# Feed-forward products in plain fp32 with one operand each, instead of fp32r high and low parts

## What is computed

```python
W_in_sim = quantize_w8_per(W_in, axis=0)      # round to 8 bit steps, one scale for each column
W_out_sim = quantize_w8_per(W_out, axis=1)    # one scale for each of the 1024 rows
x_sim = quantize_a16(x)                       # round to 1/32767 of the largest |x|
hidden = gelu(x_sim @ W_in_sim + b_in)        # 256 -> 1024
hidden_sim = quantize_a16(hidden)             # needs the largest |hidden| of all
out = hidden_sim @ W_out_sim + b_out          # 1024 -> 256
```

## Time and profile before

| | |
|---|---|
| median of 3 runs | 2500.81 us (2496.88 to 2504.37) |
| span of the profiled execution | 2491.9 us |
| TensorE busy | 1955.9 us, 78% |
| VectorE busy | 1747.3 us, 70% |
| ScalarE busy | 1316.8 us, 53% |
| GpSimd busy | 797.0 us, 32% |
| F0 | about 867 to 999 us |
| G0 | about 2109 to 2293 us |
| G1 | about 2293 to 2492 us |

### The profile page before, as it was taken

One profiled execution on the slowest core, in us unless ns is written; L12 is line 12 of the kernel. 1 busy time (PEld: TensorE's weight loads), 2 busy tenths in 40 slices (PEclk: granted clock), 3 DMA queues, 4 the chain that ended last, 5 costly groups with the idle time before them and its releaser, 6 DMA issues. The chain is left out here.

```text
span 2491.9 us, 47293 instructions
## 1 busy us (share of the span) xinstructions
PE 1955.9 (78%) x14240; PEld 1576.1 (63%) x14240; DVE 1747.3 (70%) x3674; ACT 1316.8 (53%) x2381; POOL 797.0 (32%) x866
## 2 busy tenths in 40 slices
PE   1689999999999679277788777887777775786687
PEld 0567777777777467255666666666666663665676
DVE  6567778877877378465667767767666665676788
ACT  0255666656655378144444444444444443786676
POOL 3012222222222200423333333333333332221787
PEclk9899999999999689578888888888888877898899
DMA  5576887888878100356665656666666661356565
GB/s 164 107 157 145 169 172 162 166 169 166 170 161 165 53 3 0 76 104 122 123 120 116 117 109 116 119 112 118 111 118 122 121 118 54 135 220 252 196 242 186
DMA packets 259781, 333.54 MB, mean 134 GB/s; under 512 B 29152, under 2 KB 237184, under 8 KB 251520
## 3 DMA queue, kind: packets, MB, share of 16 engines
q1 hardware_dynamic: 233088, 277.00, 49.4%
q0 software_dynamic: 26624, 55.67, 9.6%
HBM read 185.70 MB, written 144.70 MB: 133 GB/s over the span
## 5 line engine op out<-in xcount | busy, mean ns | idle before, releaser
L610 DVE TENSOR_REDUCE L_negm<-L_s_bank 128x2 f32<-128x512 f32 x1024 | 684.4, 684 | 363.2 <-PE L_s_bank L418 360.7
L475 ACT ACTIVATE L_prob<-L_t_bank 128x512 f32<-128x512 f32 x1024 | 598.9, 598 | 631.8 <-PE L_t_bank L429 625.7
L418 PE MATMUL L_s_bank<-L_kst,L_qst 96*128 96x256 f32 x2048 | 526.1, 343 | 236.5 <-DMA L_kst<-k_scratch 176.7
L418 PEld LDWEIGHTS L_s_bank<-L_kst,L_qst 96*128 96x128 f32 x2048 | 355.4, 216 | 363.0 <-issue 142.0
L429 PE MATMUL L_t_bank<-L_qst,L_kst 98*128 98x256 f32 x2048 | 460.6, 311 | 18.3 <-ACT L_prob L475 15.2
L429 PEld LDWEIGHTS L_t_bank<-L_qst,L_kst 98*128 98x128 f32 x2048 | 361.7, 217 | 33.3 <-ACT L_prob L475 30.0
L339 PE MATMUL L_o_bank<-L_prob,L_vext 128*32 128x256 f32 x4096 | 301.1, 415 | 2.7 <-ACT L_prob L475 2.7
L1289 PE MATMUL G_acc<-G_w_out,G_hhl 128*128 128x256 f32 x1024 | 140.4, 291 | 59.4 <-DVE G_hhl L1259 59.1
L259 POOL DMA_DIRECT2D L_den<-o_scratch x64 | 35.5, 554 | 452.2 <-DMA o_scratch<-L_osb 452.2
L1289 PEld LDWEIGHTS G_acc<-G_w_out,G_hhl 128*128 128x128 f32 x1024 | 127.9, 192 | 72.1 <-DVE G_hhl L1259 37.5
L339 PEld LDWEIGHTS L_o_bank<-L_prob,L_vext 128*32 128x32 f32 x4096 | 112.5, 115 | 92.6 <-issue 18.8
(11 more groups left out here) (172 smaller groups left out, 3257.2 us busy)
## 6 DMA issues: line engine op xcount, KB each, us to landing
L_qst<-q_scratch SPq DMA_DIRECT2D x384, 128.0 KB, 5.0
L_kst<-k_scratch SPq DMA_DIRECT2D x384, 128.0 KB, 6.4
q_scratch<-L_qhl SPq DMA_DIRECT2D x64, 512.0 KB, 3.0
k_scratch<-L_khl SPq DMA_DIRECT2D x64, 512.0 KB, 3.2
o_scratch<-L_osb POOLq DMA_DIRECT2D x128, 256.0 KB, 4.8
hidden_scratch<-G_hid SPq DMA_DIRECT2D x32, 1024.0 KB, 3.9
G_hid<-hidden_scratch SPq DMA_DIRECT2D x32, 1024.0 KB, 7.4
L_ctx_in<-in_ctx SPq DMA_DIRECT2D x64, 256.0 KB, 3.2
```

Of the source, the lines that this page charges most:

```text
L418: mm = pe.matmul(s_bank[k % 2][:, j, :], qst[1 - q][0:96, h, P * qt:P * (qt + 1)], kst[1 - q][0:96, h, :], start=True, stop=True)
L475: act.activation(prob[g % 2][:, k % 2, 2 * (k // 2 % 2):2 * (k // 2 % 2) + 2, :], t_bank[k % 2][:, :, :], ACT.Exp, scale=HD ** -0.5).then_ ...
L610: dve.tensor_reduce(negm[:, t, 2 * pair:2 * pair + 2, qt], s_bank[k % 2][:, :, :], AX.X, ALU.max, negate=True).then_inc(sem["dve_s"], 1)
```

## The change

F0: the tiles `xT` and the weight `cs` stay single plain fp32 tiles, so an item's product is four matmul calls instead of twelve. The low parts (L873, L850, L852) go. The normalising moves from ScalarE to GpSimd, and the statistics are written straight into `stats`.

G0: `xT` and `w_in` are single fp32 tiles, two matmul calls for an output tile instead of four. L1112 goes. Normalising moves to GpSimd, in front of the bias addition. The maximum is taken over two tiles at a time.

G1: hidden_sim is no longer multiplied by the weight's row scale; that scale goes into the weight once (`w_out`, eight VectorE instructions). ScalarE rounds four tiles in one instruction and VectorE subtracts MAGIC in place in one. One matmul call takes the place of the two. GpSimd has nothing to do. `hidden` has three load buffers instead of two.

All three stages are written out in full, without loops. The diff, cut:

```diff
-        cshl = sb("cshl", [P, 2, KT, 2 * D], F32R)
         xn = [sb(f"xn{j}", [P, NT, D]) for j in range(2)]
-        xT = [sb(f"xT{j}", [P, 2, KT, S], F32R) for j in range(2)]
+        xT = [sb(f"xT{j}", [P, KT, S]) for j in range(2)]
-        bst, mvt = sb("bst", [P, NT, 6]), sb("mvt", [P, NT, 2])
+        bst = sb("bst", [P, NT, 6])
...
+        @block.gpsimd
+        def _(pool):
+            pool.wait_ge(sem["rstd"], 4)
+            for n in range(B):
+                after(pool, sem["pe_xT"], n - 1)
...
+                for t in range(NT):
+                    tile = 2 * n + t
+                    ins = pool.tensor_scalar(xn[n % 2][:, t, :], x_res[:, tile, :], rstd[:, tile:tile + 1], nmr[:, tile:tile + 1],
+                                             ALU.mult, ALU.add)
+                ins.then_inc(sem["pool_xn"], 1)
-                        group = [(k, ca, cw) for ca, cw in ((0, 0), (0, 1), (1, 0)) for k in range(KT)]
-                        for j, (k, ca, cw) in enumerate(group):
-                            ins = pe.matmul(ri[q][:, t, :], xT[q][:, ca, k, P * t:P * (t + 1)], cshl[:, cw, k, :],
-                                            start=j == 0, stop=j == len(group) - 1)
+                        for k in range(KT):
+                            ins = pe.matmul(ri[i % 2][:, t, :], xT[i % 2][:, k, P * t:P * (t + 1)], cs[:, k, :],
+                                            start=k == 0, stop=k == KT - 1)
                     ins.then_inc(sem["pe_mm"], 1)
-            act.wait_ge(sem["rstd"], 4)
...
-                    after(act, sem["pe_mm"], i)
-                    act.activation(xT[1 - q][:, 0, :, :], tr[1 - q][:, :, :], ACT.Copy).then_inc(sem["act_xT"], 1)
-                if n_on:
-                    normalise(i + 2, q)
...
-            dve.tensor_scalar(a, a, float(np.float32(3.1415925)), -float(np.float32(3.1415925)), ALU.min, ALU.max).then_inc(sem["cs"], 4)
-            dve.tensor_copy(rstd[:, :], stats[:, :, 1]).then_inc(sem["rstd"], 1)
-            dve.wait_ge(sem["cs"], 6)
-            dve.tensor_copy(cshl[:, 0, :, :], cs[:, :, :]).then_inc(sem["cs"], 1)
-            dve.wait_ge(sem["cs"], 7)
-            dve.tensor_tensor(cshl[:, 1, :, :], cs[:, :, :], cshl[:, 0, :, :].bitcast(F32), ALU.subtract).then_inc(sem["cs"], 2)
+            dve.tensor_scalar(a, a, float(np.float32(3.1415925)), -float(np.float32(3.1415925)), ALU.min, ALU.max).then_inc(steps, 1)
...
+                if 0 <= i - 3:
+                    n = i - 3
+                    dve.wait_ge(sem["dve_bn"], n + 1)
                     for t in range(NT):
-                        ins = dve.bn_aggr(mvt[:, t, :], bst[:, t, :])
-                    ins.then_inc(steps, 1)
-                if a_on:
-                    dve.wait_ge(sem["act_xT"], i + 2)
-                    dve.tensor_tensor(xT[1 - q][:, 1, :, :], tr[1 - q][:, :, :], xT[1 - q][:, 0, :, :].bitcast(F32),
...
-            with pool.Fori(0, NCH) as i:
-                pool.wait_ge(sem["act_xn"], i + 1)
-                xr = x_res[:, bass.ds(CT * i, CT), :]
+            pool.wait_ge(sem["rstd"], 4)
+            for n in range(NCH):
+                after(pool, sem["dve_xq"], n - 1)
+                for t in range(CT):
+                    tile = CT * n + t
+                    ins = pool.tensor_scalar(xn[n % 2][:, t, :], x_res[:, tile, :], rstd[:, tile:tile + 1], nmr[:, tile:tile + 1],
+                                             ALU.mult, ALU.add)
+                ins.then_inc(sem["pool_xn"], 1)
+                pool.wait_ge(sem["pool_xn"], n + 1)
+                xr = x_res[:, CT * n:CT * (n + 1), :]
                 pool.tensor_tensor(xr, xr, b_out[:, :].unsqueeze(1).to_broadcast([P, CT, D]), ALU.add).then_inc(sem["pool_b"], 1)
...
-                    if b_on:
+                    if i >= 0:
                         after(pe, sem["act_h"], FT * i + f - 3)
-                        group = [(k, c) for c in range(2) for k in range(KT)]
-                        for j, (k, c) in enumerate(group):
-                            ins = pe.matmul(hb[f % 4][:, :], w_in[:, k, P * f:P * (f + 1)], xT[q][:, c, k, :],
-                                            start=j == 0, stop=j == len(group) - 1)
+                        for k in range(KT):
+                            ins = pe.matmul(hb[f % 4][:, :], w_in[:, k, P * f:P * (f + 1)], xT[i % 2][:, k, :], start=k == 0, stop=k == KT - 1)
                         ins.then_inc(sem["pe_h"], 1)
...
-                if a_on:
+                    dve.wait_ge(sem["pool_xn"], n + 1)
+                    dve.tensor_scalar(xq[n % 2][:, :, :], xn[n % 2][:, :, :], sx[:, 0:1], MAGIC, ALU.mult, ALU.add).then_inc(sem["dve_xq"], 1)
...
+                    for j in range(FT // 2):
+                        dve.wait_ge(sem["act_h"], FT * i + 2 * (j + 1))
+                        col = FT // 2 * i + j
+                        dve.tensor_reduce(hmax[:, col:col + 1], hid[i % 2][:, 2 * j:2 * j + 2, :], AX.XY, ALU.max,
                                           apply_absolute_value=True).then_inc(sem["dve_h"], 1)
-                    if a_on and f in (3, 4):
-                        k = f - 3
-                        dve.wait_ge(sem["act_xT"], 2 * (i + 1) + k + 1)
-                        dve.scalar_tensor_tensor(out=xT[1 - q][:, 1, k, :], in0=tr[2 * (1 - q) + k][:, :], scalar=-MAGIC,
-                                                 in1=xT[1 - q][:, 0, k, :].bitcast(F32), op0=ALU.add,
-                                                 op1=ALU.subtract).then_inc(sem["dve_xT"], 1)
...
+    LOADS = 3
-        w_out = sb("w_out", [P, FT, D], F32R)
+        w_out = sb("w_out", [P, FT, D])
         amax, wscale, winv = sb("amax", [P, FT]), sb("wscale", [P, FT]), sb("winv", [P, FT])
-        hid = [sb(f"hid{j}", [P, FT, CHUNK]) for j in range(2)]
-        hq = [sb(f"hq{j}", [P, CHUNK]) for j in range(4)]
-        hs = [sb(f"hs{j}", [P, CHUNK]) for j in range(4)]
-        hhl = [sb(f"hhl{j}", [P, 2, CHUNK], F32R) for j in range(4)]
+        hid = [sb(f"hid{j}", [P, FT, CHUNK]) for j in range(LOADS)]
+        hq = [sb(f"hq{j}", [P, FT, CHUNK]) for j in range(2)]
...
+            def load(i, half):
+                sp.dma_start(hid[i % LOADS][:, 4 * half:4 * half + 4, :], hidden[i, :, 4 * half:4 * half + 4, :]).then_inc(sem[f"h_load{i % LOADS}"], 16)
+            for i in range(LOADS):
+                for half in range(2):
+                    if half:
+                        sp.wait_ge(sem[f"h_load{i % LOADS}"], 16)
+                    load(i, half)
...
+            for i in range(NCH):
+                for half in range(2):
+                    act.wait_ge(sem[f"h_load{i % LOADS}"], 32 * (i // LOADS) + 16 * (half + 1))
+                    after(act, sem["pe_mm"], FT * (i - 2) + 4 * (half + 1))
+                    act.activation(hq[i % 2][:, 4 * half:4 * half + 4, :], hid[i % LOADS][:, 4 * half:4 * half + 4, :], ACT.Identity,
+                                   scale=scales[:, 0:1], bias=consts["magic"][:, :]).then_inc(sem["act_q"], 1)
-            chain(dve.tensor_scalar(w_out[:, :, :], w[:, :, :], -MAGIC, None, ALU.add))
+            for f in range(FT):
+                ins = dve.tensor_scalar(w_out[:, f, :], w[:, f, :], -MAGIC, winv[:, f:f + 1], ALU.add, ALU.mult)
+            chain(ins)
...
-            run(dve, step)
-            hi(dve, dve.tensor_copy, FT * NCH - 1, FT - 1, "dve_hi")
-            for f in (FT - 3, FT - 2, FT - 1):
-                lo(FT * (NCH - 1) + f, NCH - 1, f)
-            sums(NCH - 1, 1)
+            for i in range(NCH):
+                for half in range(2):
+                    dve.wait_ge(sem["act_q"], 2 * i + half + 1)
+                    part = hq[i % 2][:, 4 * half:4 * half + 4, :]
+                    dve.tensor_scalar(part, part, -MAGIC, None, ALU.add).then_inc(sem["dve_q"], 1)
+                if i >= 1:
+                    sums(i - 1)
+            sums(NCH - 1)
-                    n = FT * i + f
-                    pe.wait_ge(sem["dve_lo"], n + 1)
+                    if f % 4 == 0:
+                        pe.wait_ge(sem["dve_q"], 2 * i + f // 4 + 1)
-                        for c in range(2):
-                            ins = pe.matmul(acc[q][t][:, 0:D], hhl[f % 4][:, c, P * t:P * (t + 1)], w_out[:, f, :],
-                                            start=f == 0 and c == 0, stop=f == FT - 1 and c == 1)
+                        ins = pe.matmul(acc[i % 2][t][:, 0:D], hq[i % 2][:, f, P * t:P * (t + 1)], w_out[:, f, :],
+                                        start=f == 0, stop=f == FT - 1)
                     ins.then_inc(sem["pe_mm"], 1)
```

More of the change, by code:

```diff
@@ L761, in _ @@
         @block.tensor
         def _(pe):
-            def step(i, q):
-                n_on, a_on, b_on, c_on, s_on = stages(i)
-                if a_on:
-                    pe.wait_ge(sem["act_xn"], i + 2)
-                    after(pe, sem["dve_xT"], i)
+            for i in range(-1, B):
+                if i + 1 < B:
+                    n = i + 1
```

(4 more changed lines are left out.)

305 lines of the change are left out of this document (91 added, 214 removed).

## The result

The changed kernel takes 2640.95 us (median of 4 runs, 2636.44 to 2641.61), the kernel before 2498.85 (4 runs, 2484.88 to 2504.37). The ratio is 1.0578, with a 95% interval of 1.0547 to 1.0609. The forecast was 2642 us, in a range of 2627 to 2692. The profiled execution has a span of 2634.7 us against 2491.9 before: +142.8.

What follows compares the result with a forecast made beforehand. TensorE was taken to bound F0 and G0, the chain making high and low parts G1. Terms 21.8 - 1.5 + 79.5 - 0.2 + 49 - 8 + 1 = +141.6 on 2500.8 gave 2642 us, range 2627 to 2692.

Steps and rivals of the forecast that it cites:

- The price of a plain call: All three stages: a plain fp32 call is two instructions of two passes; 0.216 us with 256 columns, 0.430 with 512.
- F0: Cos/sin stage, 32 items: period from 3.21 to 3.89 us, +21.8; first products no longer wait, -1.5.
- the bound of 2.4: In F0, GpSimd's two tensor_scalar per item take at most 2.4 of the 3.89 us.
- G0: First quantised product, 16 chunks: period from 9.73 to 14.7 us, +79.5; start -0.7, end +0.5.
- The new edge: In G0, transposes need VectorE's rounding, now behind a two-tile maximum: 0.3 us spare, between 0 and +5, taken as 0.
- rival C: TensorE waits more, by G0's rounding, GpSimd in F0 or longer lower clock: +5 to +25, 2655; chance 9%.
- G1: Second quantised product, 16 chunks: 10.76 us between stores becomes 13.82, +49; earlier start, -8.
- the lower clock at the first chunk: G1's first chunk no longer hides the lower clock behind VectorE: 0 to +3 us, taken as +1.
- Unrolling: G1's first four chunks are already unrolled and no faster: taken as 0, between -2 and +2 us.
- A: All three stages: plain products carry the fp32r surcharge, 0.465 and 0.233 us per instruction; +44, 2686; chance 15%.
- B: A plain instruction holds TensorE no longer than an fp32r one: F0 -26, G0 -23, G1 -52; 2392; chance 4%.
- The total: Whole kernel: +141.6 us on the profiled span of 2491.9; added to the median 2500.8, 2642.

Runs made afterwards that it cites:

- two-pass kernel: The changed kernel with fp32r tiles, every product issued twice, low part left out: 2417.59 us, ratio 0.973 against the kernel before.
- four-pass kernel: The changed kernel with fp32r tiles, every product issued four times, low part left out: 2676.61 us, ratio 1.0759 against the kernel before.

## Why the prediction was right

**The price of a plain call.** Right in kind and size. Two instructions a call: 256, 512 and 1024 with 4, 16 and 32 calls per item or chunk. Two passes an instruction: 0.429 and 0.216 us where 0.430 and 0.216 were taken. The argument rested on products elsewhere in the kernel (L339, L301), on transposes, and on the earlier trace rows, where twelve fp32r products at half clock follow plain ones; the experiment with four fp32r passes carries it from the other side.

**F0.** A period of 3.873 for 3.89, so 32 x 0.666 = +21.3; the block has +20.0, so its ends gave -1.3 where -1.5 was taken. GpSimd needs 2 x 0.788 = 1.58 us of the 3.87, within the bound of 2.4, and it waits for TensorE. The bound came from a row of 512 columns.

**G0.** A period of 14.61 for 14.70: 16 x 4.88 = +78.1 where +79.5 was taken. The block has +80.0, so start and end cost +1.9 where -0.2 was taken. Two small errors offset each other. One thing that the prediction had no term for in G0 is the lower clock at the first products. In the kernel after:

```profile
2150.65 5.83 PE L940 MATMUL G_hb<-G_xT,G_w_in 128*128 128x512 f32 x8 [0.78 <-ACT G_xT L955]
```

Eight such instructions take 3.60 us in F0 at the full clock. The granted clock was 0.50 until 2155 us, so 2.2 us are lost here; in the kernel before it is 3.63 us for eight fp32r ones, which lose 1.6. That accounts for 0.6 of the difference. The rest wasn't followed further. The new edge was called one that "fits with 0.3 to spare". VectorE's timeline around one rounding in the kernel after:

```profile
2226.94 1.22 DVE L1023 TENSOR_REDUCE G_hmax<-G_hid 128x1 f32<-128x1024 f32 x1 [2.21 <-ACT G_hid L962]
2228.08 0.74 DVE L1018 TENSOR_SCALAR G_xq<-G_xn,G_sx 128x1024 f32<-128x1024 f32 x1
```

The rounding ends at 2228.82 and the transposes begin at 2229.36, in their natural place behind the products. So some 0.5 us are spare, and rival C has nothing to stand on at this edge. With two fp32r passes it binds: 12 of the 16.5 us of the two-pass kernel go with the earlier rounding.

**G1.** 13.81 a chunk, as said (+48.9 over sixteen). The start gained 8.0 us (14.6 against 22.6 from the load's issue to the first product), also as said. The timeline at G1's start in the kernel after, several engines in order of time:

```profile
2391.11 0.38 SPq L1055 DMA_DIRECT2D G_w<-in_W_out  x1
...
2402.12 2.19 DVE L1105 TENSOR_SCALAR G_w_out<-G_w,G_winv 128x256 f32<-128x256 f32 x8
...
2404.35 1.23 DVE L1120 TENSOR_SCALAR G_hq<-G_hq 128x2048 f32<-128x2048 f32 x1
...
2405.72 19.45 PE L1135 MATMUL G_acc<-G_w_out,G_hq 128*128 128x256 f32 x77 [19.80 <-DVE G_hq L1120]
```

What is last now is VectorE: eight scaled passes over the weight, then its half of the rounding queued behind them. The term that was mis-sized is the lower clock at the first chunk. The window over TensorE's first 5.3 us in the kernel after:

```profile
2405.70:2411.00 5.30, 5.28 (x13) 4.22 (x14) 2.45 (x2) 2.71 (x2) 0.00 (x0) 0.50 0.64 223
```

A granted clock of 0.50 is the lower of the two levels, 1.2 GHz, after 19.8 us in which TensorE did nothing. The first chunk's products take 16.48 us from their start to the second's, the others 13.81: 2.7 us, where +1 was taken, between 0 and +3. The kernel before had the same low stretch:

```profile
2315.69:2321.00 5.31, 5.31 (x25) 5.31 (x26) 3.94 (x7) 3.67 (x6) 5.31 (x5) 0.51 0.16 31
```

Its first chunk takes 10.11 us in spite of it, less than the period of 10.76 that the chain of the low parts sets, so the stretch is hidden there, as the prediction said. The clock's 1.7 us above the term, and 1.1 us by which the kernel before has its first and last chunks shorter than sixteen full periods, are the +2.7 by which G1's block is above the forecast's +42.

**Unrolling.** Taken as 0, between -2 and +2. In G1 with high and low parts it cost 0.1 us a chunk, 2 us in the block (200.8 against 198.8). No gain shows in F0 (3.207 either way). In G0 it wasn't tried by itself.

**The rivals.** A, the fp32r surcharge on plain products, is refuted: 0.429 and 0.216, and a sum that comes out within 2 us. B, one pass per plain instruction, would have been 2392. The two-pass kernel streams what B assumed and takes 2417, and the changed kernel is 223 us above it. B's own price was too low by more than these 25 us: by blocks it had -26 in F0, -23 in G0 and -60 in G1, and the two-pass kernel has -30.7, -4.3 and -28.7. It summed TensorE's work alone (8.3 in G0, 7.5 in G1) where a chunk takes 9.48 in G0, by the rounding edge, and 10.0 in the later part of G1, by the transfers as far as the waits tell. Attention blocks that happened to be 19 us shorter hide a part of this. C, waits on TensorE: none in steady state in any of the three windows.

**The total.** +142.8 on the span for +141.6. That it is within 2 us is partly luck. The three stages are 0.3 us below, 0.7 above and 2.7 above their terms, and the attention blocks moved by -3.9 and +1.9 on their own, where other executions have F0 begin up to 17 us earlier. What is not luck is the instruction counts and the periods, right to 0.1 us, which come out the same in the three kernels with one changed stage each.

## What to carry to other kernels

Before an exact fp32 product replaces fp32r parts, count passes: plain fp32 was four per call here, so it pays only where it removes four or more, or where TensorE has the room. Two high/low passes became four and three became four, and TensorE was 81 to 100% busy in these stages before. What the change took off the other engines was worth something by itself; it could be had without the plain products, by moving the normalising to the idle engine, rounding ahead of the last maximum and starting GpSimd early (0.9895 in all; the last alone gave 0.995, the first together with the unrolling 0.9968).

## What the runs showed of the hardware

- An fp32r pass costs 9 to 10% more than its columns, a plain one about 1%. At the full clock 512 columns are 0.2133 us. fp32r instructions of 512 columns follow at 0.233 to 0.235 (four-pass kernel), those of 256 columns at 15.02 / 128 = 0.117 instead of 0.107. A plain instruction of 256 columns, two passes, takes 0.216, one of 512 takes 0.429. The cause of the fp32r surcharge stays open: no run changed it. The Trainium skill ("TensorE: Matmul & The Clock Gate", back-to-back issue gap) gives as the gap of an isolated product at the full clock the columns over 2.4 GHz plus 2.5 ns. For 512 and 1024 streamed columns that is an estimated 0.216 and 0.429 us, and the plain products agree; the fp32r ones are 7 to 9% above it. The 131 ns that it gives for a sustained stream of 512 columns shows in no run.
- After `partition_all_reduce`, a library operation, GpSimd's first ordinary instruction comes with a pair of MODIFY_POOL_CONFIG and starts 6.7 to 9.2 us after it, with nothing else that it waits for (7.2 before G1's first in the kernel before, 7.4 in G0 of the changed one, 9.2 with the small instruction). Moved forward by a small instruction, the delay is hidden: 7.2 us at G1's start, 0.995 in time. The Trainium skill ("GPSIMD Engine Reference", section 2.1 Instruction dispatch) gives some 6 us of code load for the first call of a freshly loaded kernel, counted from MODIFY_POOL_CONFIG. The gaps here are somewhat longer. That they are such a load, paid on the way back to ordinary instructions, fits and is not shown.
- GpSimd's tensor_scalar over 256 columns has a mean of 788 ns in F0 and 566 in G0, but these are two durations mixed: of the 64 in F0, 36 take some 560 ns, with VectorE all but idle, and the other 28 some 1065 (one 1585), with VectorE busy for nearly their whole length on the sum of squares and what follows it (L824, L829, L835). In G0 even those that lie wholly beside VectorE's maximum (L1023) take some 560. So VectorE's busy share (60% and 38%) doesn't tell which it will be; the kind of instruction that runs beside it does, in these two stages. Why was not tried.
- One ScalarE instruction over 2048 columns takes 2093 ns. Three over 512 that follow each other take 2.23 us and start 0.71 apart, so four are an estimated 2.94 us.
